# A four-layer transformer chain on one core: the order of its 1326 work items taken from a table of letters instead of a list scheduler

## The reference, cut to what matters

```python
# layer 0 (and 1 with 2-D rotary on q, k; 2 with 1-D rotary, no gate)
h = layernorm(x) * (1 + scale1) + shift1
Q, K, V = h @ Wq + bq, h @ Wk + bk, h @ Wv + bv      # 16 heads of 8
x = x + gate1 * (softmax(Q K^T * s) V @ Wo + bo)
h = layernorm(x) * (1 + scale2) + shift2
x = x + gate2 * (gelu(h @ W1 + b1) @ W2 + b2)         # 128 -> 512 -> 128
# layer 3: no attention
n = where(mask, layernorm(x) * (1 + scale) + shift, 0)
x = x + gate * where(mask, gelu(n @ s1 + c1) @ s2 + c2 + gelu(n @ t1 + d1) @ t2 + d2, 0)
x = x + gate * (gelu(modulated layernorm(x) @ f1 + g1) @ f2 + g2)
```

## Time and profile before

| | |
|---|---|
| median of 3 runs | 417.49 us (415.98 to 418.70) |
| profiled execution, span from first to last instruction | 415.7 us, mean granted clock 0.979 |
| PE busy | 388.4 us (93%), 3666 instructions |
| PEld busy | 205.8 us (49%) |
| DVE, ACT, POOL busy | 329.4 (79%), 323.8 (78%), 187.5 us (45%) |
| all DMA queues | 17.63 MB, 14.7% of 16 engines' span |

### The profile page before, as it was taken

One profiled execution on the slowest core, in us unless ns is written; L12 is line 12 of the kernel. 1 busy time (PEld: TensorE's weight loads), 2 busy tenths in 40 slices (PEclk: granted clock), 3 DMA queues, 4 the chain that ended last, 5 costly groups with the idle time before them and its releaser, 6 DMA issues. The chain is left out here.

```text
span 415.7 us, 10244 instructions
## 1 busy us (share of the span) xinstructions
PE 388.4 (93%) x3666; PEld 205.8 (49%) x3670; DVE 329.4 (79%) x768; ACT 323.8 (78%) x634; POOL 187.5 (45%) x290
## 2 busy tenths in 40 slices
PE   8699899999999999999999998999999999998996
PEld 3444343455544544554545544545555444435874
DVE  6497999989886499898899874899898889935343
ACT  5207786799898968887989887769797999895664
POOL 4539999525745155453162354171451320004564
PEclk9759999999999999999999998999999999999999
DMA  7700237210005000013000023000050000000001
GB/s 254 184 15 14 78 113 203 72 32 2 2 2 149 7 6 2 2 53 103 3 6 2 2 56 98 6 2 2 2 135 20 3 2 16 2 0 3 2 0 39
DMA packets 17186, 17.63 MB, mean 42 GB/s; under 512 B 2460, under 2 KB 15454, under 8 KB 17120
## 3 DMA queue, kind: packets, MB, share of 16 engines
q1 hardware_dynamic: 15840, 16.19, 13.8%
q10 hardware_dynamic: 1296, 0.79, 0.8%
...
## 5 line engine op out<-in xcount | busy, mean ns | idle before, releaser
L1397 DVE TENSOR_REDUCE mx<-max_ps 128x1 f32<-128x512 f32 x384 | 241.9, 682 | 30.3 <-PE max_ps L908 29.2
L1223 ACT ACTIVATE probs<-exp_ps 128x512 f32<-128x512 f32 x384 | 202.6, 605 | 29.4 <-PE exp_ps L917 28.3
L908 PE MATMUL max_ps<-k_stack,q_stack 64*128 64x512 bf16 x384 | 113.5, 390 | 6.9 <-DMA k_stack<-parts 3.5
L1098 PE MATMUL pv_ps<-probs,v_ones 128*32 128x256 f32 x1536 | 103.0, 385 | 4.5 <-ACT probs L1223 3.8
L917 PE MATMUL exp_ps<-q_stack,k_stack 64*128 64x256 bf16 x768 | 101.3, 271 | 0.6 <-ACT probs L1223 0.5
L1417 POOL TENSOR_SCALAR var_eps<-mv 128x2 f32<-128x2 f32 (+2 forms) x33 | 6.5, 198 | 131.1 <-DVE mv L1257 130.0
L1098 PEld LDWEIGHTS pv_ps<-probs,v_ones 128*32 128x32 f32 x1536 | 41.1, 109 | 42.7 <-ACT probs L1223 17.2
L908 PEld LDWEIGHTS max_ps<-k_stack,q_stack 64*128 64x128 bf16 x384 | 29.4, 93 | 61.9 <-DVE mx L1397 36.2
L917 PEld LDWEIGHTS exp_ps<-q_stack,k_stack 64*128 64x128 bf16 x768 | 43.3, 94 | 29.4 <-ACT probs L1223 11.5
L1235 ACT ACTIVATE mrows<-exp_ps 8x256 bf16<-8x256 bf16 x48 | 17.5, 365 | 17.5 <-PE exp_ps L1083 17.1
L1030 PE MATMUL exp_ps<-hT,w 128*128 128x256 f32 x96 | 29.3, 425 | 0.8 <-ACT hT L1157 0.8
(11 more groups left out here) (128 smaller groups left out, 485.1 us busy)
## 6 DMA issues: line engine op xcount, KB each, us to landing
...
q_stack<-mrows SPq DMA_DIRECT2D x48, 4.0 KB
...
```

Of the source, the lines that this page charges most:

```text
L908: return pe.matmul(max_bank(n), half(q_stack, b, pair, j)[:, t * P:(t + 1) * P], half(k_stack, b, pair, j), start=True, stop=True)
L1098: mm = pe.matmul(pv_ps[32 * j:32 * j + 32, cols_of(g // 2)], v_ones[:, b, kt, 4 * g + j, :], probs[:, (4 * i + j) % RING_P, cols_of(of_two ...
L1223: act.activation(probs[:, tile % RING_P, :], exp_bank(e), ACT.Exp, scale=SCORE_SCALE[hc // 2 // NB]).then_inc(exp_read, 1)
L1397: dve.tensor_reduce(mx[:, G % 2, t, 2 * (pair % 2) + j:2 * (pair % 2) + j + 1], max_bank(n), AX_X, ALU.max, negate=True).then_inc(max_read, 1)
```

## The change

The list scheduler is removed with all its tables. `make_order` now takes the same items from named streams in the sequence of a string of 1308 letters. Each letter stands for the next item of one stream: E an EXP, m and n a MAX with j = 0 and 1, S a SPLIT, R a ROWS, P a PV, O and G OUT and OG, D one DK or DQ item, F V Z A r s x y w for FOLD, V, ZQ, ANG, RED, SIN, XG0, GATE, WARM, t the preparation of batch 1, and a to l and q the jobs (k, h): a (2,0), b (2,1), c (3,0), d (3,1), e (4,0), f (4,1), g (5,0), h (5,1), i (6,0), j (6,1), k (7,0), l and q the quarters of (7,1). SIN is a stream of its own now. The engines' programs, buffers, banks and waits are not touched. `WARM_BEATS` falls from 10 to 4; the scheduler placed 4 of its 10.

```diff
-SECOND_BATCH = 5.0
 EARLY_GATES = 1
-EARLY_ANGLES = 2
-WARM_BEATS = 10
-GATE_AFTER = 3
+WARM_BEATS = 4
...
-ENGINE_OF = {"SPLIT": "DVE", "SX": "DVE", "XH": "DVE", "MK": "DVE", "OUT": "ACT", "SIN": "ACT",
...
-SLACK = {"ROWS": -0.8, "DENSE": -0.3, "PV": 0.85, "ANG": 0.1, "EXP": 0.1, "MAX": 0.8, "NEAR": 0.15, "BESIDE": 0.5, "ALONE": 0.25, "CHANGE": 0.2, "LAST": 0.4}
-HOLD = {"61": 14, "70": 15}
+JOBS = dict(zip("abcdefghijklq", [(k, h) for k in range(NB, CHAINS + NB) for h in pieces_of(k)]))
...
+def streams():
+
+    half_jobs = range(2 * CHAINS)
+    tiles = [("MAX", hc, m) for hc in half_jobs for m in range(HALF_BEATS)]
+    table = {
+        "E": [("EXP", hc, n, j) for hc in half_jobs for n in range(HALF_BEATS) for j in range(HALVES)],
+        "m": [tile + (0,) for tile in tiles], "n": [tile + (1,) for tile in tiles],
...
+        "D": [item for k in range(1, CHAINS) for item in copies(k)],
...
+    return table | {letter: job_items(*job) for letter, job in JOBS.items()}
+
+
+ORDER_TEXT = """
+mnmnnmmnmSnmnRmntwnmyAwSmEEnErEwnmtwnREEmytEEEnmPEmEnntSmmEEnRVEmDnEntEmnEmEDSPnmEEnEPRmmSEDEEnAnmtPRnDEmEnEPEmEmnEEmESPnEDmEnER
+DPnEErmnxPOEEmnEESPmEmEnRPmEEnGEEEmPESFEEnmnrPRmEanEEnEmESaEEPRanEmnEEPEmEmEEnPamEnEmEPnOErnEEaSGEmPRmnbamnabaabmbnEEabanEmEnbZb
+ambbSmnSabbsmnRbPPEnmnaaabEmaEnmEbESnmERPRmEEEnnbbbEEEmEnPDmmEnaEEPEnbEmEEDmSPEnEEmnRPDnOEmEDEEGmESPEnDcnDEEmRFccVnEmEPEcmnmESEc
+PnnEmRccnmccnmESEcmnEEEmRPEnEEmnPEEEcmnEPmEncEEPSEnmnEEPmOEmcGRSEEnmcdEncddREEnmdEFmPPnEndmEcSddmncddnmEEdEZEdnmEEPmdEEnRPnEdcEm
+nESEmddddREDnEmEdmESPDEnEmEnPRDmEnEDEmPEnEEDmnEEnPOESEDmEnmVGEmEnRSPenEmFEmPRnEmEEnPEmEnEEeEmEnSPmEnEmERPnEmEEEPenEEmePnEEmEnPOm
+SEnEeGmERPEEnmfeeZnmfefSenmfeEnmEfRPennmfffefnEmEfefEEmnSEfneeePRmEefmEnEEnPmESEnffffREmEEemnESPmEEnmEPDRnnEEEmEPnEmEnEPmDODEfDD
+EDnEEGSmEPEngmmEEEnRPSEEmnnEVgEmEEgEnPRmngEEPmnEEmEPESEmEnmEPRnEmEgnEEmPSEEnnEmPORnmgGggmnhgEmSEnhhggmEEEnEPgmEEnRPhgmnEmhggEnEE
+nmhhnmhggShnEmESZhEhnmhERgPRnEEmPhEmEnEmhhnEhhEDDhESmEnEmPRnDEnEmEDPnmEEnEDDSPmEEnEmRPOEnmEEEGEnPimSEEEinmEEEPiRmEnEEnEPEmEEmEni
+SPEmEnmEPRiEnEEmnPEmnEEEnPSmEnEmEPORmniGimniimEEnSiiRnEmEmEEVjnmEEnEiPEmEnEnEPESmnEiEmRiPmnjiSiFnEmEEnRPmnPEmEmEnjSEPEmEEEnPREmE
+nEmPjnmOEEnEPmESEEGnEmEPREnkjmEnEmEPnEEESPREEkEkEPEEEEiEiEPkEEEFjPiPOkjjjGjqlkkjllqqlkjqkklqjlkqllklqqqjqqljljkqklijqlqkklllqjql
+jlqkjqiijjlkqkiqljqqklqlkklk
+"""
...
 def make_order():
 
-    order, at = [], {}
...
+    order = first[:2] + [("ADA0", 0, WHOLE, 0)] + first[2:]
+    order += [("ADA1", 0, WHOLE, 0)] + [("GATE", 0, WHOLE, c) for c in range(EARLY_GATES)] + [("POS", 0, WHOLE, 0)]
+    of = {letter: iter(stream) for letter, stream in streams().items()}
+    order += [next(of[letter]) for letter in "".join(ORDER_TEXT.split())]
+    assert all(next(stream, None) is None for stream in of.values())
     return order
```

More of the change, by code:

```diff
@@ L121, in exp_pair_of @@
     return 2 * (n // GROUP_BEATS) + n % 2, (n % GROUP_BEATS) // 2
-ENGINE_OF = {"SPLIT": "DVE", "SX": "DVE", "XH": "DVE", "MK": "DVE", "OUT": "ACT", "SIN": "ACT",
-             "FOLD": "POOL", "RED": "POOL", "SQ": "POOL", "XG0": "POOL", "DK": "SP", "DQ": "SP", "ZQ": "SP"}
-ARRAY = {"EXP": 0.215, "MAX": 0.215, "PV": 0.87, "ROWS": 0.12, "TR": 0.25, "OG": 0.4, "OT": 0.25, "WO": 0.45, "W1": 0.43, "W1S": 0.43,
-         "W1F": 0.43, "W2": 1.75, "W2S": 0.88, "W2F": 0.88, "K": 0.45, "Q": 0.45, "RK": 0.45, "RQ": 0.45, "V": 0.87, "ANG": 0.85,
-         "ADA1": 0.6, "GATE": 0.8, "WARM": 0.43}
-READER = {"EXP": 0.494, "ROWS": 0.3, "OUT": 0.5, "TR": 0.46, "K": 0.41, "Q": 0.41, "OT": 0.37, "V": 0.65, "W1": 0.37, "W1S": 0.37,
[3 rows of a table removed]
-PIECES = ("OT", "WO", "SX", "XH", "TR", "MK", "W1", "W2", "W1S", "W2S", "W1F", "W2F")
-SWITCH, TO_READER, TO_ARRAY, TABLE, COPY = 0.095, 0.2, 0.1, 1.28, 2.4
-AHEAD = {"DVE": 1.15, "ACT": 0.1, "POOL": 1.65, "SP": 0.95}
-SLACK = {"ROWS": -0.8, "DENSE": -0.3, "PV": 0.85, "ANG": 0.1, "EXP": 0.1, "MAX": 0.8, "NEAR": 0.15, "BESIDE": 0.5, "ALONE": 0.25, "CHANGE": 0.2, "LAST": 0.4}
-HOLD = {"61": 14, "70": 15}
+JOBS = dict(zip("abcdefghijklq", [(k, h) for k in range(NB, CHAINS + NB) for h in pieces_of(k)]))
 def with_counts(names, k, h):
@@ L150, in mlp @@
     def mlp(w):
-        names = [w] * CHUNKS[w]
-        if (k, w) == (NB, "W1") and h == 0:
-            names.append("SIN")
-        return names + ["W2" + w[2:]]
+        return [w] * CHUNKS[w] + ["W2" + w[2:]]
     names = ["OT", "WO", "SX", "XH", "TR"] + mlp("W1") + ["SX", "XH", "TR"]
@@ L160, in job_items @@
         names += ["MK"] + mlp("W1S") + ["SX", "XH", "TR"] + mlp("W1F")
[L161 removed]
+    return with_counts(names, k, h)
 def gelu_of(name, layer):
     return "GELU" if name == "W1S" or (name == "W1" and layer == 1) else "TANH"
[L169 to L385 removed]
@@ L389, in make_order @@
-    for item in first:
-        order.append(item)
-    order.extend([("ADA1", 0, WHOLE, 0)] + [("GATE", 0, WHOLE, c) for c in range(EARLY_GATES)] + [("POS", 0, WHOLE, 0)])
-    streams.append([("GATE", 0, WHOLE, c) for c in range(EARLY_GATES, 3)])
-    at.update({("DQ", 0, WHOLE, 2): 0.0, ("V", 0, WHOLE, 0): -3.0, ("split", "RK", 0, WHOLE): -3.0, ("split", "SQ", 0, WHOLE): -3.0,
-               ("POS", 0, WHOLE, 0): 10.0})
-    max_no[0] = 2 + EARLY_GATES
-    streams.append(with_counts(["ST", "XH", "TR", "K", "Q", "SQ"], 1, WHOLE))
@@ L397, in make_order @@
-    streams.append([("WARM", n, 0, 0) for n in range(WARM_BEATS)])
-    streams.append([("V", 1, WHOLE, 0)])
-    streams.append(with_counts(["DK"] * 3 + ["DQ"] * 3, 1, WHOLE))
-    heads = [0] * len(streams)
-    def partner(item, start, others):
-        name, k, h, c = item
-        if name == "EXP" and c == 0 and len(exp_read) >= EXP_BANKS - 1 and exp_read[1 - EXP_BANKS] + TO_ARRAY <= start + 0.1:
-            return True
-        if name == "MAX" and half_pair[0] is None and bank_read[(max_no[0] + 1) % MAX_BANKS] + TO_ARRAY <= start + 0.1:
-            return True
-        return any(r[2][0] in ("EXP", "MAX") and r[2][0] != name and r[2][3] != c and r[0] <= start + 0.1 for r in others)
@@ L411, in slack @@
-    def slack(item, start, others):
-        name = item[0]
-        if name in ("EXP", "MAX"):
-            beside = shape[0] == 64 and array[1 - item[3]] > max(start, array[item[3]]) + 0.05
-            favour = SLACK["BESIDE"] if beside else 0.0 if partner(item, start, others) else -SLACK["ALONE"]
-            if name == "EXP":
-                return free["ACT"] - start - ARRAY["EXP"] - TO_READER - SLACK["EXP"] - favour
-            return free["DVE"] - start - ARRAY["MAX"] - TO_READER - SLACK["MAX"] - favour
-        kind = 32 if name == "PV" else 128
-        return SLACK.get(name, SLACK["DENSE"]) - (SLACK["CHANGE"] if shape[0] == kind else 0.0) + (SLACK["LAST"] if item[1] >= CHAINS and name in PIECES else 0.0)
```

242 lines of the change are left out of this document (10 added, 232 removed), and 3 rows, old and new, of the table READER.

## The result

The changed kernel takes **380.44 us** (median of 4 runs, 378.27 to 380.69), beside 418.1 for the kernel before in the same session: a ratio of 0.909, 95% interval 0.905 to 0.913. The forecast was 404.5 with a range of 397 to 414. The gain is 37 us where 13 were forecast.

A forecast was written before the change was run, and what follows sets the result against it. PE was taken as the bound, with 27.8 us hidden waits and 27.3 us visible idle. Terms -3.0 - 5 - 2.5 - 2.5 + 0 = -13.0 gave a span of 402.7, median 404.5 us, range 397 to 414.

The forecast's parts named there:

- What bounds the kernel: PE, 93% busy: 27.8 us of waits hidden in score runs beside 27.3 us visible idle, some 55 us to win.
- Score runs and changes of kind: On PE: 168 score runs instead of 185, 419 slots instead of 422, fewer other changes of kind; -3.0 us.
- chain ends: Where one layer's chain gives way to the next: earlier last splits keep DVE supplied, one clock dip goes; -2.5 us.
- Bank waits: MAX and EXP products waiting until their bank is read: unavoidable waits fall from 24.5 to 10.3 us; -5 taken, bound -14.
- uses closer than three reductions: MAX bank uses under 1.83 us apart only fall from 186 to 181; a reason for taking a third of the gain.
- no hole of 10 us between MAX: Sign of being right at the first chain end, beside DVE at more than 7.2 us of 15.
- Opening: Start of the kernel: earlier SPLIT and ROWS bring the first EXP 3.8 us earlier; -2.5 us, bounds +1 and -4.
- the 32 us: Opening's clock: still at 0.5 beyond 32 us was a sign of being wrong.
- Tail: After the last PV: 26.4 us of PE items instead of 25.0, filling idle time; 0 us, bounds -3 and +3.
- Nearly all waits go: Rival: bank waits come off in full and the clock holds at 2.4 GHz; -24 us, 395 us; chance 0.14.
- SP's queue as the gate: Rival: ROWS copies stuck in SP's queue behind copies of unsplit parts; slower, 422 us; chance 0.08.
- a mark of failure: Sign of being wrong: waits of line 833 or 799 in SP's queue for POOL above 10 us.

The follow-up runs named there:

- g1: The changed kernel's order with the half 0 product first in every beat of MAX, so 84 pairs exchange places: 386.4 us (0.922).
- e3: The changed kernel's order with every item that is not attention, except WARM, moved back by four units of attention work, about half a microsecond: 449.5 us (1.078).
- e4: The order before, items moved up to ten places until no use of a bank comes too soon after the one it must wait for: 555.5 us (1.328).
- f2: The order before, improved by a search moving one item at a time, judged over the whole order by the removed scheduler's tables: 402.4 us (0.963).
- f3: The order before, items moved at most ten places, judged by a reckoning of the whole chain in the traces' durations: 407.9 us (0.975).
- f4: The changed kernel's order, searched over any distance with the traces' durations: 403.7 us (0.965).
- g2: The changed kernel's order, searched within eight places by fitted durations, first 112 items left alone and the pairing kept: 388.7 us (0.929).
- g3: The order before, searched over any distance with durations and delays fitted to the runs so far, pairing among them: 403.3 us (0.964).
- h1: The order before, searched with fitted durations, its opening left as it was and SP's wait for POOL's gates counted: 397.8 us (0.950).
- e6: The changed kernel's order with the last two jobs, last OUT and OG and what they need at the earlier kernel's places, first 748 items untouched: 399.95 us (0.954).
- g4: The changed kernel's order with GATE, ANG and two warming products moved behind the first six EXP: 382.5 us (0.914).

## Why the prediction was wrong, step by step

**What bounds the kernel.** Right, and the best part of it: waits hide in the busy time, and the score runs hold 27.8 us of them. After holds 12.6. "That is all an order can win, some 55 us" was right in kind too: 27 of them were won. Dense products and ROWS gave 7 more, which that sum had taken for work.

**Score runs and changes of kind, -3.0.** The counted part is -2.5, and g1 shows that such slots go to the end one for one. The dense and ROWS runs fell by another 7.4, of which 1.5 is the clock's dip that is gone (counted with the chain ends). Of the rest the forecast had 0.5, for other changes of kind. Waits hidden inside dense and ROWS runs, as in score runs, are the likeliest reading, and I had not counted them at all; no run separates them.

**Bank waits, -5 of at most -14. This is the step that failed.** I had counted 24.5 us of unavoidable waiting before and 10.3 after, beside measured 27.8; measured after is 12.6, a change of -15.1, three times the -5 and beyond the bound of -14. The count was good and the cut to a third was not. Its reason was that DVE cannot be pressed harder and that uses closer than three reductions hardly fall. The windows show DVE going from 88% to 95% of the middle, by waiting less for PE, not by working more.

**The term that was absent.** 11.8 us of PE's visible idle time went (2.3 of them in the tail), where the steps for chain ends and opening together took off 5 and the tail nothing. The rivals stopped at -24 because I looked for named places (one chain end, one dip, one opening). The idle time fell by 1.1 to 2.6 us in each of seven stretches, so the order acts on many hand-overs. e3, e4, f2 and f3 speak for one cause, the distance of every item to what it waits for, in PE, ACT, DVE, POOL and SP alike: a small shift of all of it costs 69 us, and a reckoning of the whole chain wins where a rule on banks alone loses. As a forecast that theory was still off: of the searches it judged, f2, f3, f4, g2, g3 and h1 all came slower than it had said.

**Chain ends, -2.5.** Right in kind: no hole of 10 us between MAX, DVE at 13.5 of 15 us, no dip. Its size cannot be told apart from the terms above.

**Opening, -2.5.** Wrong in sign: +3.9 at OUT 0, of which 2 may be this execution's clock (e6). ROWS moved as forecast, but EXP waited behind 5.9 us of dense products at 1.2 GHz, and g4 shows that even an EXP in the forecast place gains nothing. The clock stood at 0.50 to 37.1, beyond the 32 us that the prediction had named as a sign of being wrong, and for this step it was one. The fault was to count an engine's earlier start as a gain without asking what the same PE time was then late for.

**Tail, 0.** -3.1, at the lower bound; with the late jobs at before's places e6 has before's tail again, 38.6 us. 2.3 of the 3.1 are visible idle time of PE.

**The rivals.** "Nearly all waits go" was the nearest and still 13 to 15 us short (393.5 by its sum, 395 as stated); it named the right mechanism and had 0.14. The Trainium skill's rule that it leaned on (Perfetto Trace Analysis, Identifying the Most-Contended Engine: matmul busy share is no measure of closeness to the limit, weight-load share is) would have said most of all that 93% of PE leaves room; by that rule, the trace agrees: with the same 205.8 us of weight loads the time fell by 9%, and their share went from 49% to 54%. SP's queue as the gate did not happen, though its sign did. The waits of SP's queue and of EXP in after:
```profile
SPq L542 <- POOL parts L1187: 11.7, 5, 5.9
```
```profile
PEld exp_ps L660 <- DMA q_stack<-mrows: 0.6, 2, 0.4
```
SP waits longer for split parts than in the earlier trace rows, at five places and above the 10 us that the prediction had called a mark of failure, but the EXP behind the copies waited 0.6 us in all. In g3 the queue did cost 9.4 us, at the gates and not at the splits. The range's lower end, 397, left out what the bounds of the parts allowed (-29.4, which is 388), and the measured time lies below that too.
